# Attention, last unit: two more PSUM banks for the scores, two left for heads, projection, gate and experts

## What is computed

```python
attn = jnp.einsum('bqhd,bkhd->bhqk', q, k) * scale
attn = jnp.where(causal, attn, jnp.float32(-jnp.inf))
attn = jax.nn.softmax(attn, axis=-1)
out = jnp.einsum('bhqk,bkhd->bqhd', attn, v).reshape(B, S, C)
...
h = x + _gqa(_rmsnorm(x, attn_norm_w), wq, wk, wv, wo)
out = h + _moe(_rmsnorm(h, ffn_norm_w), gate_w, expert_w)
```

## Time and profile before

| | us |
|---|---|
| median of 3 runs | 1411.52 (1410.43 to 1412.02) |
| the profiled execution | 1413.26 |
| its span, first to last instruction | 1411.9 |
| PE busy | 1145.6 (81%) |
| DVE busy | 1088.2 (77%) |
| ACT busy | 717.8 (51%) |
| POOL busy | 743.6 (53%) |

### The profile page before, as it was taken

One profiled execution on the slowest core, in us unless ns is written; L12 is line 12 of the kernel. 1 busy time (PEld: TensorE's weight loads), 2 busy tenths in 40 slices (PEclk: granted clock), 3 DMA queues, 4 the chain that ended last, 5 costly groups with the idle time before them and its releaser, 6 DMA issues.

```text
span 1411.9 us, 18716 instructions
## 1 busy us (share of the span) xinstructions
PE 1145.6 (81%) x5568; PEld 534.8 (38%) x5568; DVE 1088.2 (77%) x2980; ACT 717.8 (51%) x1535; POOL 743.6 (53%) x973
## 2 busy tenths in 40 slices
PE   3513797899999997686666778999999999999885
PEld 1201345455555544332322233343333434433232
DVE  5889655575788888779898859788989889888027
ACT  4644677126544435433221135675667557755771
POOL 7524485355777778765674026525462545264423
PEclk9855898899999998887776569999999999999997
DMA  4000100522211110002223140202011302000002
GB/s 117 0 0 0 51 1 5 147 81 66 58 43 42 51 32 22 0 0 44 29 65 37 36 66 6 53 14 43 14 27 13 43 14 38 3 4 1 3 2 59
DMA packets 33683, 47.04 MB, mean 33 GB/s; under 512 B 5023, under 2 KB 18207, under 8 KB 33279
## 3 DMA queue, kind: packets, MB, share of 16 engines
q1 hardware_dynamic: 30990, 43.84, 14.0%
q10 hardware_dynamic: 2592, 2.00, 0.5%
HBM read 39.14 MB, written 6.68 MB: 32 GB/s over the span
## 4 chain that ended last, share of the span: by engine, by line
PE 34%; DVE 19%; ACT 4%; issue 3%; POOL 2%; DMA 0%; ACTq 0%; DVEq 0%; POOLq 0%
PE PS L695 9%; PE PS L626 7%; PE PS L678 6%; DVE PS L1194 4%; PE PS L741 4%; DVE SS L1197 4%; DVE RB L1128 3%; PE PS L337 2%; DVE st L784 1%; ACT RB L1673 1%; PE PS L538 1%; DVE PS L1108 1%; PE PS L557 1%; DVE B L1128 1%; DVE PS L1183 1%
## 5 line engine op out<-in xcount | busy, mean ns | idle before, releaser
L1673 ACT ACTIVATE RB<-PS 128x512 f32<-128x512 f32 (+3 forms) x768 | 322.5, 499 | 175.3 <-PE PS L678 171.8
L626 PE MATMUL PS<-B 96*128 96x512 bf16 (+3 forms) x768 | 248.7, 350 | 38.6 <-DVE SS L1194 12.5
L1194 DVE CUSTOM_DVE_ANT_0 PS<-PS,w_msk 128x128 f32<-128x128 f32 (+3 forms) x512 | 242.5, 504 | 20.4 <-PE PS L626 19.9
L678 PE MATMUL PS<-B 96*128 96x512 bf16 (+3 forms) x768 | 236.0, 330 | 11.3 <-ACT RB L1673 10.5
L2021 POOL TENSOR_SCALAR_AFFINE_SELECT RB<-RB 128x512 f32<-128x512 f32 x128 | 81.1, 637 | 252.7 <-ACT RB L1673 252.7
L1197 DVE TENSOR_REDUCE SS<-PS 128x1 f32<-128x512 f32 x256 | 175.4, 685 | 34.0 <-PE PS L626 32.2
L695 PE MATMUL PS<-RB,B 128*32 128x512 f32 (+3 forms) x1536 | 165.0, 503 | 1.3 <-POOL RB L2021 1.3
L626 PEld LDWEIGHTS PS<-B 96*128 96x128 bf16 x768 | 75.1, 100 | 223.0 <-DVE SS L1194 97.2
L1851 POOL TENSOR_TENSOR RB<-RB,B 128x512 f32<-128x512 f32 x64 | 82.4, 1289 | 86.7 <-DVE RB L1022 64.1
L678 PEld LDWEIGHTS PS<-B 96*128 96x128 bf16 x768 | 73.3, 98 | 91.0 <-ACT RB L1673 62.1
L1515 ACT ACTIVATE RB<-PS 128x512 f32<-128x512 f32 x72 | 42.8, 596 | 127.1 <-PE PS L440 127.0
(11 more groups left out here) (270 smaller groups left out, 2213.7 us busy)
## 6 DMA issues: line engine op xcount, KB each, us to landing
B<-scrW SPq DMA_DIRECT2D x128, 128.0 KB, 3.1
B<-scrQ SPq DMA_DIRECT2D x72, 128.0 KB
scrQ<-B SPq DMA_DIRECT2D x6, 384.0 KB, 2.6
B<-scrK SPq DMA_DIRECT2D x36, 64.0 KB
X<-in_x SPq DMA_DIRECT2D x8, 256.0 KB, 8.5
out_dram<-X SPq DMA_DIRECT2D x7, 256.0 KB, 3.2
B<-in_w SPq DMA_DIRECT2D x3, 576.0 KB, 4.8
B<-in_zeros SPq DMA_DIRECT2D x9, 128.0 KB
```

The costliest lines, as they stand in the source:

```text
L626: pe.matmul(p[:, 0:w], qs[u % 3][:, h, 128 * i:128 * i + 128], keys_of(u, h)[:, 512 * c:512 * c + w], start=True, stop=True).then_inc(s["m ...
L678: pe.matmul(p[:, 0:w], keys_of(u, 4 * kl + z)[:, 128 * kt:128 * kt + 128], qs[u % 3][:, 4 * kl + z, 512 * qc + off:512 * qc + 512], start= ...
L1194: ins = dve.tensor_tensor_reduce(p, p, msk[:, 512 - w:512], 1.0, LOWEST, ALU.add, ALU.max, MX[:, u % 2, i, h, c:c + 1])
L1673: act.activation(RB[:, 4 * (step % 3) + z, 0:w], bank(bank_of["score", step, z])[:, 0:w], ACT.Exp).then_inc(s["ex2"], 1)
```

## The change

From step 166 (`SCORES_ALONE`) a score takes its bank from five, 0 to 4, in place of three, and until step 197 the ring has two banks, 5 and 6, in place of four. `heads_2` is given the step, so that it takes its bank by the same rule. From step 197 on the ring is the same as before. Nothing is added, removed or moved in any engine's program.

```diff
+        SCORES_ALONE = 166
...
                 if step >= POST_AT[NG - 1]:
                     return (3, 4, 5, 6, 0, 1, 2)[ring_1[0] % 7]
+                if step >= SCORES_ALONE:
+                    return 5 + ring_1[0] % 2
                 return 3 + ring_1[0] % 4
...
-                k = (4 * step + z) % 3
+                k = (4 * step + z) % (3 if step < SCORES_ALONE else 5)
...
-            def heads_2(n):
+            def heads_2(step, n):
                 pe.wait_ge(s["os2"], n + 1)
-                k = next_1(0)
+                k = next_1(step)
...
-                        heads_2(n)
+                        heads_2(step, n)
```

## The result

| | before | after |
|---|---|---|
| median of the first comparison, us | 1410.23 (6 runs, 1407.67 to 1412.02) | 1401.51 (6 runs, 1398.83 to 1403.75) |
| ratio | | 0.9933 (95% interval 0.9915 to 0.9951) |
| span of the profiled execution | 1411.9 | 1401.0 |
| median of all executions of the study | 1411.10 (118) | 1401.87 (30) |

The kernel is faster, by 8.7 us by the first medians, by 9.4 us (6.9 to 12.0) by the ratio, and by 9.6 us by the means of all executions (1411.37 and 1401.73; standard errors 0.25 and 0.41). Forecast were 7.0 us and 1404.5; the range ended at 1402.3. In the four comparisons that timed both kernels side by side the means lie 8.8, 10.1, 8.7 and 9.9 us apart. The kernel before runs 1405 to 1418 us from execution to execution (standard deviation 2.7), so only pooled executions, or a cut of the traces, tell 7 from 9.

The account below looks back on a forecast made before the run. The prediction took a latency loop between PE's scores and ACT's exponentials to bound the kernel. Gains of 1.6 + 3.0 + 2.5 - 0.1 = 7.0 us, taken from a median of 1411.52, gave 1404.5 us, range 1402.3 to 1408.7.

Parts of the forecast that it names:

- The loop of the full step: Full steps: the fourth score waits for its own step's first exponential; five banks cut 2.40 us to 1.96.
- ACT and PE nearly equal, part of the gain lost: Rival, 15%: in full steps, PE at 1.96 and ACT at 1.95 us delay each other; half the gain, 1408.0 us.
- The segments of unit 7: Steps 168 to 175, 176 to 183 and 184 to the experts of 190 gain 1.6, 3.0 and 2.5 us.
- Two banks for the ring: Experts of step 191 wait for DVE's last reads of step 190's banks: 0.1 us lost, nothing counted elsewhere.
- Start: Steps 166 and 167 win nothing, because step 168 waits for the guard's transfer and begins at 1320.00 us as now.
- this case: Sign of being wrong: step 168 earlier than 1319 us, the guard no anchor, 0.4 to 0.8 us more won.
- The tail: From the experts of step 190 to the end: as long as now, 40.2 us.
- its clock: Rival, 6%: PE's clock in the tail falls elsewhere; up to 2.2 us less, 1402.3, or about 4 more, 1408.5.
- The time outside the span: Whole execution: time 1413.26 with span 1411.9 us becomes time 1406.3 with span 1404.9.
- The range: Whole kernel, 1402.3 to 1408.7 us: half the gain and the clock either way, without no gain and slower.
- the highest case: Tail, part of the 6% clock rival: all 16 expert rows at half clock, about 4 us more, 1408.5 us.

Follow-up runs that it names:

- four_banks: The changed kernel with four banks for the scores instead of five and three for the ring, from step 166; ratio 0.9928 to the kernel before.
- ring_two: The kernel before with only the ring cut to two banks from step 166, scores still at three; ratio 0.9998.
- the pair: The kernel before and the changed kernel, each with idle matmuls in PE's waits of the tail; means of all executions 1407.63 and 1399.95 us.
- after_warm: The changed kernel with idle matmuls filling PE's waits in the tail; first median 1399.72 us.
- before_d: The kernel before, repeated without an edit; median 1412.19 us.
- from_162: The changed kernel with the switch to five score banks at step 162 instead of 166; ratio 0.9926 to the kernel before.
- from_168: The changed kernel with the switch to five score banks at step 168 instead of 166; ratio 0.9950 to the kernel before, median 1402.74 us.

## Why the prediction was wrong

Two terms that the sum had put at nothing were not nothing, the start and the tail; the terms that it worked out were right.

*The loop of the full step*: right, and shown by four_banks to be the whole of what the steps win; 1.97 us against 1.96. *ACT and PE nearly equal, part of the gain lost*: this rival did not happen; ACT runs four steps without a gap. *The segments of unit 7*: 1.56, 2.98 and 2.39 against 1.6, 3.0 and 2.5. *Two banks for the ring*: 0.15 against 0.1, by the wait for `mx_h` that was named, and none elsewhere (ring_two).

*Start* is the step that failed by reading: "I take step 168 to begin at 1320.00 as now", because the list of waits has 0.6 us of the weight load for the transfer. That engine's idle time lay under a product; PE did not wait. Steps 166 and 167 win 0.65 us on the mean. The text priced this case itself, 0.4 to 0.8, but left it out of the sum.

*The tail* was set at no change, and its clock given 6% as a rival. The rival's premise holds in every trace of the kernel before: the clock falls there, at a cost of 2.4 to 3.5 us. How much it costs varies, and the changed kernel has on the mean 0.8 us less of it by the traces, 2 us less by what the idle matmuls take off (3.7 from the kernel before, 1.8 from the changed one; the difference is uncertain by 0.9). A term that moves by 2 us from trace to trace belongs in the range of every case, not in a case of its own.

*The time outside the span* was taken to stay as it is (1413.26 less 1411.9, then 1406.3 less 1404.9: 1.4 us). The changed kernel has 1.45, but the kernel before has 2.14 on the mean, and its profiled execution was one of the short ones. Why it shrinks is open.

*The range* carried the uncertainty of the sum and none of the measurement: executions of one kernel scatter by 2.7 us, a median of six by more than 1 us. The measured median lay 0.8 us below its lower end. Of the 3.0 us between 1404.5 and 1401.5, 1.3 come from the kernel before, whose median was 1411.52 by three executions and 1410.23 by six; that part is chance. The other 1.7 are gain that was not forecast. The upper end, 1408.7, is 0.2 above the highest case that it is said to cover, 1408.5.

By the traces the sum is 6.93 - 0.15 + 0.65 + 0.8 = 8.2 us, against 9.0 us inside the span by the executions, both uncertain by about half a microsecond; with the 0.7 us outside it that makes the whole. The 0.8 us left between 8.2 and 9.0 are not clear of this uncertainty. With equal tails the spans of the pair lie 7.4 us apart and the stages give 7.1, so the rest may be more of the tail's clock; it isn't shown, and may be chance. That the clock falls less far in the changed kernel because its PE was busier before is argued only, not shown.

## What to carry to other kernels

Where items per step and banks are such that the last item of a step shares a bank with the first of the same step (4 on 3 here), producer and consumer run one behind the other; one more bank opened this here, and a fifth brought nothing. Other numbers of banks and items were not tried. Idle time of the weight load is no wait of the engine: look whether a matmul row covers it before taking a transfer for an anchor. When a kernel's executions scatter by more than the change is worth, cut each trace at marks of the program: the steps from 168 to the experts of step 190 repeat to 0.03 us while the total scatters by 13. And look at how much of a time lies outside the span before subtracting spans from times.

## What was not expected of the hardware

With identical programs up to step 164, the time to the guard's copy was anything from 1308.4 to 1315.2 us in the nine traces of the two kernels. The guard's transfer landed 3.06 us after its issue in one trace of the changed kernel, 3.88 us in one of after_warm. In the tail PE's granted clock is 0.50 for 3 to 7 us at a time after PE has stood between small pieces of work (before PE's last work it falls once in most traces, twice in before_d, four_banks and from_162), and a few idle matmuls of 0.2 us each keep it at 1.00, which takes off 2.4 to 3.5 us of the kernel before by the traces and 3.7 us by the executions. The time of an execution outside its span differs between kernels whose last instructions are the same: 1.4 us in every execution of from_168 and four_banks, as in the changed kernel, and up to 3.4 us in the kernel before.
